# Constant and bias rows from GpSimd's queue, the lists of VectorE and GpSimd behind the T step in another order, and the gates of the T step one slot later

## The chip, the core and the metric

The kernel runs on one core of a Trainium2 chip. The core has TensorE (PE in the rows), VectorE (DVE), ScalarE (ACT), GpSimd (POOL) and SyncE (SP), which here only issues transfers. Each engine works through its own list in order, and they wait for one another through semaphores. The metric is device time in microseconds (us), the median of several runs. Lower is better.

## What is computed

The input x is 8 batches of 128 channels by 256 positions. Self-attention with 16 heads of 8 channels runs on each batch, with a mask on the keys; its result goes through a gated feed-forward block whose activations are rounded to 8-bit integers and whose weights are rounded to -1, 0 or 1; the output of that is added to x.

```
Q, K, V = (proj(Wq), proj(Wk), proj(Wv))
att = einsum('bhqd,bhkd->bhqk', Q, K) / sqrt(8) + b
att = softmax(att * mask + (1 - mask) * NEG_INF)
y = einsum('bhqk,bhkd->bhqd', att, V)
...
h = silu(bit_linear(y, w_gate)) * bit_linear(y, w_up)      # I = 1024
h = rms_norm(h, ln_weight)
out = x + bit_linear(h, w_down)
# bit_linear: activations rounded by their row's maximum, weights by their mean
```

## The kernel before

**Attention, steps n = -1 to 8 of 8 slots (k) each.** Query and key are split into three bf16 parts and stacked over 88 of 128 rows, so that one bf16 matmul gives scores of near float32 accuracy. Batch b lives in `q_st[b % 4]` and `k_st[b % 4]`; the parts get there by small transfers ("high" part 0, "low" parts 1 and 2). Besides the parts a stack has constant rows (ones, or zeros where the maxima will stand) and bias rows (the mask). In slot (n, k) TensorE makes the scores of batch n+1 (`scores`), whose maxima VectorE takes with one reduction a slot (line 938), and the transposed scores of batch n (`scores_t`, the T units), whose exponentials ScalarE takes in two instructions a slot (line 578), and the products with the values (`values`, line 1061). GpSimd turns the maxima into negated bf16 rows (`negate_maxes`), TensorE transposes them (line 1072, at k = 2 and k = 6), ScalarE copies them (line 601), and SyncE moves them into the query stack (line 350). `scores_t` at k = 1 and k = 5 waits for that transfer. Between its pieces of attention GpSimd rounds the weights in steps 4 to 6 (`quantize_weights`, lines 481, 485 and 489, two or three instructions at a time).

**The T step, n = 7 and the start of n = 8.** No scores of a next batch are left. In the place of them units of the feed-forward block run: unit u = 2b + f is half f of batch b. `gate(u)` and `up(u)` are two matmuls each (line 1152); ScalarE takes a tanh or silu of the gate (lines 667 and 676); VectorE multiplies (lines 853, 861, 872, giving `hid`). With one pair of banks for units up to 6, `gate(u)` waits until unit u-1 has been taken out of its bank. `slot_number` s is 0 to 11; before, `gate(s/2)` stands at the end of the even slots, `up` at the end of the odd ones.

**Behind the T step.** For each batch VectorE makes `hid` twice, the upper half of `hw = hid * ln` (line 881, GpSimd makes the lower half, line 512), the row maximum of `hw` (`hidden_maximum`, line 887), the steps of rounding (`hidden_steps`, lines 896 to 900) and the residual (line 917). GpSimd makes the root mean square's inverse and a limit from ScalarE's mean (`hidden_rms`, lines 520 and 522) and the rounding (`round_hidden`, line 530). TensorE transposes that (line 1171), ScalarE copies it (line 700), and `down` (line 1191) gives the output. For the last batch of attention, `scale_y(7)` on VectorE (lines 827, 830, 833) and `quantize_y(7)` on ScalarE (line 610) finish its 8-bit input, and `scale_late_tokens` makes the scales of batches 6 and 7.

All lists are written out by hand; the order in the code is the order on the engine. A number in brackets of a name, as in `hidden_steps(1)`, is the batch.

## Time and profile before

| | us |
|---|---|
| median of 3 runs | 168.88 (168.17 to 168.94) |
| the profiled execution, its own time | 168.71 |
| its span | 166.9 |
| mean granted TensorE clock, share of full speed | 0.969 |

The profiled execution lies 0.17 us below the median, and 1.8 us of its time lie outside the span. The stretches are: start and first scores 0 to 26 us, steps of attention of about 11.6 us each up to 109 us, the T step to about 130 us, the feed-forward block of the remaining batches to the end.

### The profile page before, as it was taken

To read this page: it belongs to the slowest core of one execution; us is meant where nothing else is said; L and a number is where in the kernel's file an instruction comes from. 1 tells how busy PE (TensorE), PEld (TensorE's weight loads), DVE (VectorE), ACT (ScalarE), POOL (GpSimd) and SP (SyncE) were. 2 spreads that over 40 slices of the span, in tenths; PEclk is the share of its full clock that TensorE was granted. 3 is DMA by queue.
4 is the path that set the end of the run, shared out by engine and by line. 5 is a ranking of instruction groups with operands and counts; after the bars stand their busy time and mean duration, and the time that the engine had idled before them with its cause. 6 is when DMAs were issued, how large, how long until landed. Compare 5 with 4: busy or idle time off the path is not lost.

```text
span 166.9 us, 4106 instructions
## 1 busy us (share of the span) xinstructions
PE 147.3 (88%) x1395; PEld 68.8 (41%) x1402; DVE 137.3 (82%) x199; ACT 125.3 (75%) x255; POOL 98.7 (59%) x181
## 2 busy tenths in 40 slices
PE   6969996998999999999999999988789757999883
PEld 3645553433333433433443333323123323766772
DVE  6789997497999989789898998953679666999972
ACT  3041468599899899889889888878699937598970
POOL 5889618508608618508889869523052559779930
PEclk9999999699999999999999999999999995699999
DMA  3984996636246236623322000000000000010112
GB/s 117 299 180 122 266 246 200 161 77 199 57 109 189 45 80 197 182 71 100 76 72 70 0 3 7 5 4 5 0 0 4 0 2 0 0 35 31 33 63 94
DMA packets 20124, 14.19 MB, mean 85 GB/s; under 512 B 2160, under 2 KB 19080, under 8 KB 20104
## 3 DMA queue, kind: packets, MB, share of 16 engines
q1 hardware_dynamic: 17480, 11.76, 25.2%
q10 hardware_dynamic: 2624, 2.17, 4.9%
q8 instruction: 11, 0.18, 0.5%
q14 instruction: 9, 0.07, 0.2%
HBM read 6.17 MB, written 1.07 MB: 43 GB/s over the span
## 4 chain that ended last, share of the span: by engine, by line
PE 61%; ACT 13%; issue 7%; DVE 7%; POOL 5%; ACTq 2%; DMA 2%; DVEq 0%; POOLq 0%
PE y_ps L1061 14%; PE s_ps L1022 13%; ACT probs L578 8%; PE t_ps L1041 6%; PE s_ps L1152 5%; PE t_ps L1171 4%; PE t_ps L998 3%; PE t_ps L1082 3%; PE y_ps L1102 2%; POOL h_m L530 2%; ACTq L286 2%; PE y_ps L1191 2%; PE t_ps L1007 2%; DMA q_st<-nm_rows 2%; PE t_ps L1191 2%
## 5 line engine op out<-in xcount | busy, mean ns | idle before, releaser
L938 DVE TENSOR_REDUCE maxes<-s_ps 128x4 f32<-128x1024 f32 x64 | 75.8, 1217 | 7.8 <-PE s_ps L1022 7.6
L578 ACT ACTIVATE probs<-t_ps 128x512 f32<-128x512 f32 x118 | 65.9, 591 | 10.0 <-PE t_ps L1041 7.8
L1041 PE MATMUL t_ps<-q_st,k_st 64*128 64x256 bf16 x236 | 43.0, 276 | 4.6 <-ACT probs L578 1.9
L1022 PE MATMUL s_ps<-k_st,q_st 64*128 64x256 bf16 x256 | 45.3, 276 | 0.1
L1061 PE MATMUL y_ps<-probs,v_pad 128*18 128x256 f32 x512 | 39.1, 388 | 0.2 <-ACT probs L578 0.2
L1022 PEld LDWEIGHTS s_ps<-k_st,q_st 64*128 64x128 bf16 x256 | 15.9, 94 | 29.0 <-issue 14.7
L1152 PE MATMUL s_ps<-w_q,ffn_x 128*128 128x512 bf16 x59 | 17.5, 396 | 7.3 <-DVE hid L872 4.4
L445 POOL TENSOR_SCALAR nm_parts<-maxes 128x16 bf16<-128x16 f32 x16 | 3.3, 209 | 29.7 <-DVE maxes L938 24.0
L1041 PEld LDWEIGHTS t_ps<-q_st,k_st 64*128 64x128 bf16 x236 | 14.0, 94 | 9.5 <-ACT probs L578 4.3
L512 POOL TENSOR_TENSOR hw<-hid,ln_bc 128x512 f32<-128x512 f32 x8 | 10.2, 1272 | 12.3 <-DVE hid L861 10.4
L1061 PEld LDWEIGHTS y_ps<-probs,v_pad 128*18 128x18 f32 x512 | 9.6, 96 | 13.9 <-issue 11.7
L530 POOL TENSOR_SCALAR h_m<-hw,h_qs 128x1024 f32<-128x1024 f32 x7 | 9.2, 1310 | 5.0 <-DVE h_qs L899 5.0
L1152 PEld LDWEIGHTS s_ps<-w_q,ffn_x 128*128 128x128 bf16 x64 | 4.9, 99 | 16.7 <-issue 12.4
L1171 PE MATMUL t_ps<-ident_f,h_m 128*128 128x128 f32 x64 | 10.4, 294 | 1.3 <-ACT h_T L700 0.5
L700 ACT ACTIVATE h_T<-t_ps 128x512 bf16<-128x512 f32 x16 | 9.1, 596 | 3.2 <-PE t_ps L1171 3.1
L683 ACT ACTIVATE hid_sq<-hid 128x1024 f32<-128x1024 f32 x8 | 8.5, 1056 | 3.8 <-DVE hid L872 3.8
L586 ACT ACTIVATE qk_f<-t_ps 128x512 f32<-128x512 f32 x7 | 4.2, 597 | 9.1 <-PE t_ps L998 5.3
L887 DVE TENSOR_REDUCE h_amax<-hw 128x1 f32<-128x1024 f32 x8 | 9.7, 1208 | 1.4 <-POOL hw L512 1.3
L1171 PEld LDWEIGHTS t_ps<-ident_f,h_m 128*128 128x128 f32 x64 | 8.0, 151 | 4.0 <-issue 2.1
L472 POOL TENSOR_TENSOR parts<-qk_r,parts 128x512 bf16<-128x512 f32 x7 | 8.1, 1160 | 0.6
L468 POOL TENSOR_TENSOR qk_r<-qk_f,parts 128x512 f32<-128x512 f32 x7 | 8.1, 1157 | 0.6
L872 DVE TENSOR_TENSOR hid<-silu_g,s_ps 128x512 f32<-128x512 f32 x12 | 8.1, 678 | 0.2 <-ACT silu_g L676 0.2
(114 smaller groups left out, 242.7 us busy)
## 6 DMA issues: line engine op xcount, KB each, us to landing
q_st<-parts SPq DMA_DIRECT2D x48, 64.0 KB
k_st<-parts SPq DMA_DIRECT2D x33, 64.0 KB
w_f<-in_wgT ACTq DMA_DIRECT2D x2, 512.0 KB, 5.4
w_f<-in_wuT SPq DMA_DIRECT2D x2, 512.0 KB, 4.1
w_f<-in_wdT SPq DMA_DIRECT2D x2, 512.0 KB, 4.3
out<-o_sb SPq DMA_DIRECT2D x8, 128.0 KB, 1.7
k_st<-parts ACTq DMA_DIRECT2D x15, 64.0 KB
x_sb<-in_x SPq DMA_DIRECT2D x2, 256.0 KB, 3.7
```

Of the source, the lines that this page charges most:

```text
L512: pool.tensor_tensor(hw[:, b % 3, 0:512], hid[:, b % 2, 0, :], ln_bc[:, 0:512], ALU.mult)\
L530: pool.tensor_scalar(h_m[:, b % 3, :], hw[:, b % 3, :], h_qs[:, b:b + 1], MAGIC, ALU.mult, ALU.add)\
L578: act.activation(probs[:, t % NP_RING].rearrange("p e t -> p (e t)"), src, ACT.Exp, scale=SCALE)\
L683: act.activation(hid_sq[:, :], hid[:, b % 2].rearrange("p f n -> p (f n)"), ACT.Square, accum_out=h_ssq[:, b:b + 1]).then_inc(sq_done, 1)
L700: act.activation(h_T[:, b % 2, 4 * f:4 * f + 4].rearrange("p a t -> p (a t)"), t_bank(f), ACT.Copy, bias=-MAGIC).then_inc(hT_copied, 1)
L887: dve.tensor_reduce(h_amax[:, b:b + 1], hw[:, b % 3, :], AX.X, ALU.max, apply_absolute_value=True)\
L938: dve.tensor_reduce(dst[:, :, s, :], s_ps[:, c % 2], AX.X, ALU.max).then_inc(s_maxed, 1)
L1022: mm = pe.matmul(s_ps[:, c % 2, i, e, :], q_st[b % RING][rows, hp, qt * P:qt * P + P], k_st[b % RING][rows, hp, :], start=True, stop=True)
L1041: mm = pe.matmul(t_bank(bank["t", t])[:, e * T:e * T + T], k_st[b % RING][rows, hp, kt * P:kt * P + P], q_st[b % RING][rows, hp, :], start ...
L1061: last = pe.matmul(y_ps[32 * j:32 * j + HEAD_COLS, tau * T:tau * T + T], v_pad[:, b, kt, a, (DH + 1) * s:(DH + 1) * s + HEAD_COLS], probs[ ...
L1152: last = pe.matmul(s_ps[:, slot(u), m].rearrange("p a t -> p (a t)"), ffn_x[:, a, b, :], w_q[:, m, a * I + 512 * f:a * I + 512 * f + 512], ...
L1171: last = pe.transpose(t_bank(f)[:, c * P:c * P + P], h_m[:, b % 3, 512 * f + c * P:512 * f + c * P + P], ident_f[:, :])
```

## The change

- SyncE gives up the constant and the bias rows of batches 3 to 7. GpSimd issues them, two transfers a batch, at the end of steps 0 to 4, behind `negate_maxes(n + 1, 0)` (in step 4 ahead of two instructions of rounding weights). They count on semaphores of their own. Rows of batch 2 stay on SyncE, both ahead of the high part.
- `load_high` takes over the waits that a stack is free or cleared.
- The gates of units 1 to 5 move from the end of slot 2u to slot 2u+1, behind its T units and transposes and ahead of its products with the values.
- VectorE: `hidden_steps(1)` ahead of `hidden_maximum(2)`; `scale_y(7)` behind the second half of batch 3; `scale_late_tokens` comes from GpSimd to VectorE right behind it, with five instructions for six.
- ScalarE: `quantize_y(7)` behind the silus of batch 4.

```diff
-LOADS = 2 * len(SPLITS) + 2
+LOADS = 2 * len(SPLITS)
...
         def load_high(queue, b, side):
+            if b >= RING:
+                queue.wait_ge(unit_ready, unit["t", 16 * (b - RING + 1) - 1] + 1)
+            elif b:
+                queue.wait_ge(q_zeroed, b + 1)
+                queue.wait_ge(k_zeroed, b + 1)
             queue.wait_ge(hi_ready, b + 1)
...
+            def load_constant_rows(b):
+                if b < RING:
...
+                    pool.dma_start(q_st[b % RING][BIAS_ROWS], ones6[:, :, :].to_broadcast([6, NHP, T]))\
+                        .then_inc(later_rows_in[b % RING], 16)
+                else:
+                    pool.wait_ge(unit_ready, unit["t", 16 * (b - RING + 1) - 1] + 1)
+                    pool.dma_start(q_st[b % RING][MAX_ROWS], zeros6[:, :, :].to_broadcast([6, NHP, T]))\
+                        .then_inc(later_rows_in[b % RING], 16)
+                pool.wait_ge(bias_stored, 16)
+                pool.dma_start(k_st[b % RING][BIAS_ROWS],
...
                 if has(n + 1):
                     negate_maxes(n + 1, 0)
+                if n >= 0 and has(n + 3):
+                    load_constant_rows(n + 3)
                 for step in weight_steps.get(n, ((), ()))[1]:
                     quantize_weights(step)
...
                         if u == 5:
                             weight_high_half(2)
+                            hidden_steps(1)
...
             hidden_maximum(AHEAD - 1)
-            scale_y(B - 1)
-            hidden_steps(AHEAD - 2)
             for b in range(AHEAD, B):
                 gate_times_up(2 * b)
                 hidden_steps(b - 1)
                 gate_times_up(2 * b + 1)
                 weight_high_half(b)
+                if b == AHEAD:
+                    scale_y(B - 1)
+                    scale_late_tokens()
...
+                    s = slot_number(n, k)
+                    if s > 1 and s % 2:
+                        gate(s // 2)
                     if not has(n + 1):
                         due_values(n, k)
...
-                    s = slot_number(n, k)
-                    if s >= 0 and s % 2 == 0:
-                        gate(s // 2)
+                    if s == 0:
+                        gate(0)
                     if s >= 0 and s % 2:
                         up(s // 2)
```

GpSimd's list at the end of step 4 and the start of step 5 was, with `nm_parts` and `nm_t` the instructions of `negate_maxes` and `w_f`, `w_q` those of rounding weights:

```order
L453 TENSOR_SCALAR nm_parts<-nm_t 128x4x4 [waits nm_step]
L481 TENSOR_SCALAR w_f<-w_f,w_inv 128x2048 [waits abs_done,wscale_step]
L485 TENSOR_SCALAR w_f<-w_f 128x2048 [waits w_rounded]
L445 TENSOR_SCALAR nm_parts<-maxes 128x4x4 [waits unit_ready,s_maxed]
L447 TENSOR_TENSOR nm_t<-maxes,nm_parts 128x16 [waits nm_step]
```

and is now:

```order
L446 TENSOR_SCALAR nm_parts<-nm_t 128x4x4 [waits nm_step]
L494 DMA q_st<-zeros 6x8x256 [waits unit_ready]
L497 DMA k_st<-bias_scr 6x8x256 [waits bias_stored]
L474 TENSOR_SCALAR w_f<-w_f,w_inv 128x2048 [waits abs_done,wscale_step]
L478 TENSOR_SCALAR w_f<-w_f 128x2048 [waits w_rounded]
L438 TENSOR_SCALAR nm_parts<-maxes 128x4x4 [waits unit_ready,s_maxed]
L440 TENSOR_TENSOR nm_t<-maxes,nm_parts 128x16 [waits nm_step]
```

Two transfers now stand ahead of the weights and of the next `negate_maxes`.

VectorE's list behind the T step was, from the upper half of `hw` of batch 2 on:

```order
L881 TENSOR_TENSOR hw<-hid,ln_bc 128x512 [waits hid_done]
L887 TENSOR_REDUCE h_amax<-hw 128x1 [waits high_product,low_product]
L827 TENSOR_REDUCE y_amax<-t_ps 128x1 [waits unit_ready]
L830 TENSOR_SCALAR y_step<-y_amax 128x1 [waits yq_scale]
L833 RECIPROCAL y_qs<-y_step 128x1 [waits yq_scale]
L896 TENSOR_SCALAR h_step<-h_amax,h_lim 128x1 [waits amax_done,hs_pool]
L899 RECIPROCAL h_qs<-h_step 128x1 [waits step_done]
```

and is now, from the same place on and then from `hw` of batch 3 on:

```order
L887 TENSOR_TENSOR hw<-hid,ln_bc 128x512 [waits hid_done]
L902 TENSOR_SCALAR h_step<-h_amax,h_lim 128x1 [waits amax_done,hs_pool]
L905 RECIPROCAL h_qs<-h_step 128x1 [waits step_done]
L906 TENSOR_SCALAR h_os<-h_step,h_rs,u_down 128x1
L893 TENSOR_REDUCE h_amax<-hw 128x1 [waits high_product,low_product]
L878 TENSOR_TENSOR hid<-silu_g,s_ps 128x512 [waits low_product,sq_done,up_ready,silu_done]
```

```order
L887 TENSOR_TENSOR hw<-hid,ln_bc 128x512 [waits hm_done,hid_done]
L820 TENSOR_REDUCE y_amax<-t_ps 128x1 [waits unit_ready]
L823 TENSOR_SCALAR y_step<-y_amax 128x1 [waits yq_scale]
L826 RECIPROCAL y_qs<-y_step 128x1 [waits yq_scale]
L847 TENSOR_SCALAR u_scale<-y_step,w_mean 128x2 [waits yq_scale]
L848 TENSOR_SCALAR u_eps<-y_qs,w_inv 128x2
L850 TENSOR_SCALAR g_scale<-y_step,w_mean 128x2
L852 SCALAR_TENSOR_TENSOR u_sq<-u_scale 128x2 [waits late_scales]
L854 TENSOR_SCALAR u_down<-u_scale,w_mean 128x2
L893 TENSOR_REDUCE h_amax<-hw 128x1 [waits high_product,low_product]
```

The three instructions of `hidden_steps(1)` went ahead of a maximum, and eight small ones now stand between `hw` and the maximum of batch 3.

TensorE's list in slots 4 and 5 of the T step was, with `q_st,k_st` the T units and `w_q,ffn_x` the gate and the up of unit 2:

```order
L1061 MATMUL y_ps<-probs,v_pad 18x256 x3
L1152 MATMUL s_ps<-w_q,ffn_x 128x512 [waits gated,unit_free2]
L1152 MATMUL s_ps<-w_q,ffn_x 128x512
L1041 MATMUL s_ps<-q_st,k_st 128x256 [waits unit_free4,nm_in1]
L1041 MATMUL t_ps<-q_st,k_st 128x256 [waits unit_free0]
L1041 MATMUL s_ps<-q_st,k_st 128x256
L1041 MATMUL t_ps<-q_st,k_st 128x256
L1096 MATMUL t_ps<-ident_f,y_m 128x128 [waits unit_free0,unit_free2]
L1096 MATMUL t_ps<-ident_f,y_m 128x128
```

and is now:

```order
L1073 MATMUL y_ps<-probs,v_pad 18x256 x3
L1053 MATMUL s_ps<-q_st,k_st 128x256 [waits unit_free4,nm_in1]
L1053 MATMUL t_ps<-q_st,k_st 128x256 [waits unit_free0]
L1053 MATMUL s_ps<-q_st,k_st 128x256
L1053 MATMUL t_ps<-q_st,k_st 128x256
L1108 MATMUL t_ps<-ident_f,y_m 128x128 [waits unit_free0,unit_free2]
L1108 MATMUL t_ps<-ident_f,y_m 128x128
L1164 MATMUL s_ps<-w_q,ffn_x 128x512 [waits gated,unit_free2]
L1164 MATMUL s_ps<-w_q,ffn_x 128x512
```

The gate went behind four T matmuls and two transposes.

## Rows read from the trace of the kernel before

**Rows 1.** The page: TensorE's granted clock in 40 slices, tenths of full speed.
```profile
PEclk9999999699999999999999999999999995699999
```

**Rows 2.** Stretches: length, busy PE, PEld, DVE, ACT, POOL, clock, DMA share, GB/s.
```profile
90.90:102.50 11.60, 11.28 (x143) 4.45 (x142) 10.86 (x14) 10.24 (x22) 9.66 (x15) 1.00 0.02 4
```
```profile
130.00:140.00 10.00, 5.94 (x30) 2.94 (x30) 6.83 (x17) 6.04 (x13) 6.34 (x13) 0.89 0.00 1
```

**Rows 3.** Timeline, start: start, length, engine, line, what, [idle before <- releaser].
```profile
23.00 0.36 ACT L601 ACTIVATE nm_rows<-t_ps 24x256 bf16<-24x256 bf16 x1
...
23.39 0.75 SPq L350 DMA_DIRECT2D q_st<-nm_rows  x1
...
26.28 0.28 PE L1041 MATMUL t_ps<-q_st,k_st 64*128 64x256 bf16 x1 [1.26 <-DMA q_st<-nm_rows]
```

**Rows 4.** Transfers by line: ns of issue (smallest/median/largest), first and last start, us.
```profile
L331 SPq DMA_DIRECT2D q_st<-ones x4: 777/790/941, 3.2 to 21.7; - x4
```
```profile
L350 SPq DMA_DIRECT2D q_st<-nm_rows x16: 714/764/791, 23.4 to 115.3; - x16
```

**Rows 5.** Timeline, GpSimd at the end of a step, and around step 5.
```profile
49.88 0.20 POOL L445 TENSOR_SCALAR nm_parts<-maxes 128x16 bf16<-128x16 f32 x1 [4.80 <-DVE maxes L938]
```
```profile
84.50 1.89 POOL L485 TENSOR_SCALAR w_f<-w_f 128x2048 f32<-128x2048 f32 x1
...
86.59 0.21 POOL L445 TENSOR_SCALAR nm_parts<-maxes 128x16 bf16<-128x16 f32 x1 [0.21 <-DVE maxes L938]
...
87.79 0.20 POOL L453 TENSOR_SCALAR nm_parts<-nm_t 128x16 bf16<-128x16 f32 x1
...
88.33 0.28 PE L1072 MATMUL t_ps<-ident_b,nm_parts 128*24 128x128 bf16 x2
...
88.97 2.36 DVE L938 TENSOR_REDUCE maxes<-s_ps 128x4 f32<-128x1024 f32 x2 [0.18 <-PE s_ps L1022]
```

**Rows 6.** Timeline, the T step.
```profile
118.58 0.38 PE L1152 MATMUL s_ps<-w_q,ffn_x 128*128 128x512 bf16 x1 [1.25 <-DVE silu_g L853]
...
119.31 0.60 ACT L578 ACTIVATE probs<-s_ps 128x512 f32<-128x512 f32 x1 [1.57 <-PE t_ps L1041]
...
130.72 0.36 DVE L815 RECIPROCAL y_rec<-t_ps 128x32 f32<-128x32 f32 x1 [1.14 <-PE t_ps L1082]
```

**Rows 7.** Timeline, VectorE and GpSimd behind the T step.
```profile
132.96 1.22 DVE L887 TENSOR_REDUCE h_amax<-hw 128x1 f32<-128x1024 f32 x1
...
134.10 0.41 DVE L827 TENSOR_REDUCE y_amax<-t_ps 128x1 f32<-128x256 f32 x1
...
134.82 0.21 DVE L896 TENSOR_SCALAR h_step<-h_amax,h_lim 128x1 f32<-128x1 f32 x1
...
135.32 1.12 POOL L530 TENSOR_SCALAR h_m<-hw,h_qs 128x1024 f32<-128x1024 f32 x1 [2.25 <-DVE h_qs L899]
...
137.44 0.21 DVE L896 TENSOR_SCALAR h_step<-h_amax,h_lim 128x1 f32<-128x1 f32 x1 [1.45 <-POOL h_lim L522]
...
137.95 0.68 DVE L872 TENSOR_TENSOR hid<-silu_g,s_ps 128x512 f32<-128x512 f32 x1
...
138.66 0.69 DVE L881 TENSOR_TENSOR hw<-hid,ln_bc 128x512 f32<-128x512 f32 x1
...
139.36 1.26 POOL L512 TENSOR_TENSOR hw<-hid,ln_bc 128x512 f32<-128x512 f32 x1
...
140.65 1.22 DVE L887 TENSOR_REDUCE h_amax<-hw 128x1 f32<-128x1024 f32 x1 [1.31 <-POOL hw L512]
```

**Rows 8.** Timeline, five small VectorE instructions: the first and the fifth.
```profile
109.53 0.22 DVE L838 TENSOR_SCALAR g_scale<-y_step,w_mean 128x6 f32<-128x6 f32 x1
...
110.20 0.22 DVE L845 TENSOR_SCALAR u_down<-u_scale,w_mean 128x6 f32<-128x6 f32 x1
```

**Rows 9.** Timeline, the next batches behind the T step.
```profile
143.93 1.61 DVE L881 TENSOR_TENSOR hw<-hid,ln_bc 128x512 f32<-128x512 f32 x1
...
145.86 1.20 DVE L887 TENSOR_REDUCE h_amax<-hw 128x1 f32<-128x1024 f32 x1
```

82 lines of the change are left out of this document (37 added, 45 removed).

## The prediction

> **What bounds the kernel now.** I read the stretches first. In a steady step of 11.60 us VectorE is busy for 10.86 us [rows 2], more than ScalarE and GpSimd; TensorE's 11.28 us are pipelined matmuls with modelled ends and say less. The reader is to see there that VectorE's maxima set the pace of a step, and that an edit which doesn't reach VectorE (or TensorE just ahead of it) is worth nothing in this stage. Behind the T step the picture is another: from 130 to 140 us nobody is busy for more than 6.83 of 10 us [rows 2], so engines wait for each other in a circle. Then the timelines of the three places that the change touches: the first maxima's transfer [rows 3], GpSimd at the ends of steps [rows 5], and the lists of VectorE and GpSimd behind the T step [rows 7]. Last the clock: TensorE is at its upper level (2.4 GHz) but for one slice near 30 us and two from 138 to 146 us [rows 1], where the mean share is 0.6, 0.5 and 0.6.
>
> **SyncE gives up transfers: 0 to -0.5 us, I take -0.1.** On SyncE an issue of the ones costs 0.79 us by the median [rows 4], and I price the bias rows alike, 1.58 us a pair. In the steady steps no row of the views shows TensorE waiting for the stack for longer than its usual gap, and VectorE sets the pace, so these 1.6 us a step are bought from an engine that nobody waits for. At the start the transfer of the first maxima is on the path: TensorE waits 1.26 us for it until 26.28 us. But SyncE issues it at 23.39 us, right behind ScalarE's copy (23.00 + 0.36 = 23.36 us) [rows 3], so the issue can't be earlier. What can change is the landing, 26.28 - 23.39 = 2.89 us with issue, since one transfer fewer is in flight ahead of it. Above I know nothing that makes it longer; below I allow 0.5 us of the 1.26 us. The waits that `load_high` takes over are for events that the rows transfers waited for before.
>
> **GpSimd issues two transfers a batch: +1.5 us, in step 4 alone.** No row of the trace has a transfer issued by GpSimd. The nearest row is the same transfer on SyncE: 1.58 us the pair by the median, and 2 x 0.94 = 1.88 us by the slowest issue of ones [rows 4]. I call the pair D. At the ends of steps 0 to 3 GpSimd then stands idle for `negate_maxes`, 4.80 us in the row [rows 5], which hides any D up to that. In step 4 it has two weight instructions behind the pair. They end at 84.50 + 1.89 = 86.39 us, and GpSimd had only 0.21 us of idle time ahead of the next `negate_maxes`, which ends at 87.79 + 0.20 = 87.99 us; TensorE transposes its result at 88.33 us, in order, ahead of the second half of the scores of that slot; VectorE waits 0.18 us for these and goes on at 88.97 us [rows 5]. So the cover is 0.21 us and at most 0.34 us of handing over, of which I count 0.14 us: a delay of D - 0.35 us goes through TensorE to VectorE, and VectorE, which sets the pace, doesn't get it back. With D = 1.88 us that is 1.53 us. I take the slowest row, since a pair on an engine that issues nothing else is rather like the first than like the median. The bounds: D as low as nothing, if the issue doesn't hold up GpSimd's arithmetic, gives 0; D = 2.9 us gives 2.55 us. That upper end is GpSimd's slowness against VectorE for the same multiplication (1.26 against 0.69 us [rows 7], 1.83 times), put on 1.58 us. Behind it GpSimd is late by D and TensorE by D - 0.35 us, so at the next `negate_maxes` the two stand 0.35 us nearer than before, and no second stall of size comes.
>
> The Trainium skill, page "DMA: Bandwidth & Descriptors", section "Latency and other measured facts", gives about 1 us until the first byte of a transfer from GpSimd, because its cores make the descriptors in software, against about 0.6 us on the other queues. No row here shows it; by that figure D would be an estimated 2.0 us and the delay 1.65 us, and the sum below would end 0.1 us higher. The same page ("Issuing engines are not separate DMA queues") says that issuing from more engines saves only the time of issue, which speaks against this part of the change.
>
> **Gates of the T step a slot later: -0.4 us.** Before, TensorE stands at gate(2) until 118.58 us because VectorE has not taken unit 1 (1.25 us idle); the T units queued behind it keep ScalarE waiting 1.57 us until 119.31 us [rows 6]. Now these T units go first. They wait for the last maxima's transfer, issued at 115.3 us [rows 4]; with the 2.89 us of [rows 3] it lands at about 118.2 us, so ScalarE starts the exponentials near 118.6 us, 0.7 us earlier. Against this each gate is behind four T matmuls, and TensorE's list gets full: gate, products, up and the next T units follow without a gap from about 122.7 us. I walked the list on and kept 0.25 us at the last exponentials and 0.4 us at VectorE's `y_rec`, which stood at 130.72 us after 1.14 us idle [rows 6]. Bounds: -0.8 us (all of the early start kept, and a little more for the transpose of batch 6 that no longer stands behind a gate) and +0.9 us (a gate late by the T units in each of the last units).
>
> **VectorE's and GpSimd's lists: -2.2 us.** The circle before: the maximum of batch 2 (from 132.96 us), `scale_y` (134.10 us), `hidden_steps(1)` (134.82 us), GpSimd's rounding (135.32 us, after 2.25 us idle), its root and limit, `hidden_steps(2)` (137.44 us, after 1.45 us idle), `hid` of unit 7 (137.95 us), its `hw` (138.66 us). Meanwhile GpSimd does the late scales and only then, at 139.36 us, the lower `hw` of batch 3, for which VectorE's next maximum waits 1.31 us until 140.65 us [rows 7].
> - `hidden_steps(1)` goes past a maximum and `scale_y`: 134.82 - 132.96 = 1.86 us earlier, plus the 0.4 us of the T step, so it starts near 132.6 us.
> - The circle behind it keeps its length (137.95 - 134.82 = 3.13 us to `hid` of unit 7), since GpSimd was waiting for exactly this: unit 7 at about 135.7 us, its `hw` done at 135.7 + 0.68 + 0.7 = 137.1 us.
> - `scale_y` (134.82 - 134.10 = 0.72 us) and the late scales stand there now. Five like instructions took 110.20 + 0.22 - 109.53 = 0.89 us [rows 8]. The maximum of batch 3 starts at 137.1 + 0.72 + 0.89 = 138.7 us. GpSimd's lower `hw` can start at about 135.2 us without the late scales ahead of it and is done by then; the wait of 1.31 us is gone. Gain at this point 140.65 - 138.7 = 1.95 us, 0.4 us of it the T step's.
> - From this maximum to the next the kernel took 145.86 - 140.65 = 5.21 us [rows 9, 7], of which 1.61 us are a `hw` that takes 0.69 us where GpSimd's rounding doesn't run beside it [rows 9, 7]. GpSimd's rounding of batch 3 now starts earlier against it, and ScalarE and TensorE are ahead by the same shift. I count 0.65 us of the 0.92 us, since two engines that alternate will still meet somewhere. Behind it the batches repeat, and the gain is carried to the end.
>
> That is 1.55 + 0.65 = 2.2 us beside the 0.4 us. Bounds: 1.2 us (nothing of the last point, 0.35 us lost to a collision) to 2.6 us.
>
> **The sum** against the profiled execution's own 168.71 us: -0.1 + 1.53 - 0.4 - 2.2 = -1.2 us, 167.5 us. The median of before lies 0.17 us above that execution, which is less than the error of any term, and I leave the number as it is.
>
> **The rivals.**
> - GpSimd's arithmetic is not held up by the pair, or so little that 0.35 us cover it. For it: nothing in the trace shows the contrary. Against it: transfers hold up SyncE for 0.71 us and more each [rows 4]. It gives 168.71 - 2.7 = 166.0 us.
> - Slower: the pair is dear. If D is 3.5 us or more, TensorE stands still for over 3 us in step 5, and its clock falls behind that. Such a thing is seen at the start: a wait of 1.26 us until 26.28 us [rows 3] is followed by the slice at 0.6 [rows 1]. Price: 3.2 us, plus 1 us for a slice at the lower level, less 2.7 us: 170.2 us. It decides from D = 4.1 us, or 3.1 us with the fall of the clock (168.71 - 2.7 + D - 0.35 past 169.7 us, less that 1 us); from there the kernel is slower by over 0.5%.
> - The tail gives most back. TensorE stays at the lower level from 138 to 146 us as before [rows 1], and VectorE's upper `hw` of batch 3 now meets GpSimd's rounding of batch 2, as that of batch 4 did at 143.93 us for 1.61 us instead of 0.69 us [rows 9, 7]. Then 0.9 us and 0.9 us of the 2.6 us are lost: 167.5 + 1.8 = 169.3 us, or 168.4 us with one of the two.
> - The T step gets longer: the later gates cost 0.9 us instead of giving 0.4 us, 168.8 us.
>
> The Trainium skill, page "SBUF — State Buffer", section "Who interferes with whom", has VectorE instructions with two inputs in SBUF and GpSimd's reads lock each other out for a whole instruction; by that rule the second of two that meet waits, whichever it is, which the 1.61 us agree with, and the collision is a matter of where the two lists stand.
>
> **How the numbers follow.** A measurement of this kernel can tell about 0.5%, 0.84 us, from no change; so faster is below 168.0 us and slower above 169.7 us. Forecast 0.41 (166.8 to 168.2 us; 0.34 of it faster, 0.07 same). Pair hidden 0.20 (165.4 to 166.6 us, 0.19 faster). Pair dear 0.16 (169.4 to 172 us, 0.15 slower). Tail gives back 0.15 (168.4 to 169.3 us, 0.02 beyond on the slow side). T step longer 0.08 (same). Faster 0.34 + 0.19 = 0.53, slower 0.15 + 0.02 = 0.17, the rest 0.30. The range leaves out the lowest 0.05 of the second case and nearly all of the third: 165.6 to 169.5 us.
>
> **What would show it.** The pair: GpSimd's row of `negate_maxes` in step 5 later than its maxima, a wait of TensorE's transpose (line 1072 before) for it of about 1.5 us, and a step longer by that. The gates: exponentials of pair 60 waiting under 1 us and `y_rec` nearer to the last step of attention than the 21.2 us from 109.53 to 130.72 us. The lists: GpSimd's first rounding behind the T step about 2.3 us earlier against `y_rec`, no wait of the maximum of batch 3 for GpSimd, and 13 us instead of 15.1 us from `y_rec` to the maximum of batch 4. What would make it wrong: an issue on GpSimd of under 0.3 us or over 1.5 us, a fall of the clock in a place where none was, or a wait of ScalarE's silu of batch 4 that moves into the place of the one removed.

## The result and the profile after

The changed kernel took 163.74 us (median of 4 executions, 162.91 to 165.66), beside 168.52 us for the kernel before (median of 4, 167.66 to 168.94). The ratio is 0.971, 95% interval 0.962 to 0.979. Here and below all executions count in the medians and ranges, while those over 1.5% above the fastest of the same kernel are left out of the ratios. The forecast was 167.5 us, in a range from 165.6 to 169.5 us: the sign was right, the size was not, and the time lies below the range. The profiled execution took 163.05 us, 5.66 us less than that of before, and its span is 161.2 us instead of 166.9.

The page of the changed kernel: granted clock, and the DMA queue that is new (packets, MB, share of 16 engines).

```profile
PEclk9999999999999999999999999999999999999999
...
q0 software_dynamic: 320, 0.25, 1.0%
```

Two things are seen. GpSimd's transfers are there (q0, 320 packets). And TensorE's clock, which before fell in a slice near 30 us and in two from 138 us on [rows 1], doesn't fall at all in this execution. Whether the change did that is half of the story below.

The same stretches as in [rows 2], of the changed kernel: length, busy PE, PEld, DVE, ACT, POOL, clock, DMA share, GB/s.

```profile
90.00:101.60 11.60, 11.28 (x142) 4.45 (x142) 11.09 (x14) 10.24 (x22) 10.15 (x15) 1.00 0.01 3
128.00:138.00 10.00, 6.75 (x42) 3.87 (x41) 8.94 (x24) 7.29 (x16) 7.16 (x10) 1.00 0.00 1
```

The steady step is what it was. In the ten microseconds behind the T step VectorE is now busy for 8.94 us instead of 6.83: the circle of waits is partly undone.

The timeline of the changed kernel around step 5, GpSimd and VectorE (against [rows 5]): start, length, engine, line, what, [idle before <- releaser].

```profile
80.78 0.62 POOL L494 DMA_DIRECT2D q_st<-zeros  x1
81.41 0.56 POOL L497 DMA_DIRECT2D k_st<-bias_scr  x1
...
86.04 0.21 POOL L438 TENSOR_SCALAR nm_parts<-maxes 128x16 bf16<-128x16 f32 x1
...
87.59 0.27 PE L1084 MATMUL t_ps<-ident_b,nm_parts 128*24 128x128 bf16 x2 [0.86 <-POOL nm_parts L446]
...
88.22 2.35 DVE L944 TENSOR_REDUCE maxes<-s_ps 128x4 f32<-128x1024 f32 x2 [1.10 <-PE s_ps L1034]
```

The pair is 0.62 + 0.56 us of GpSimd's time. GpSimd has no idle left ahead of the maxima of step 5, TensorE waits 0.86 us for its result, and VectorE 1.10 us instead of 0.18 us for TensorE. The chain is the one that was forecast, the price is not.

The T step of the changed kernel (against [rows 6]):

```profile
114.24 0.72 SPq L350 DMA_DIRECT2D q_st<-nm_rows  x1
...
116.12 1.21 ACT L570 ACTIVATE probs<-s_ps 128x512 f32<-128x512 f32 x2
...
116.30 0.28 PE L1053 MATMUL s_ps<-q_st,k_st 64*128 64x256 bf16 x1
...
117.22 0.59 ACT L570 ACTIVATE probs<-t_ps 128x512 f32<-128x512 f32 x1
...
128.21 0.36 DVE L808 RECIPROCAL y_rec<-t_ps 128x32 f32<-128x32 f32 x1 [1.14 <-PE t_ps L1094]
```

The first T unit that needs the last maxima starts 2.06 us after their transfer was issued, without a wait. Its exponential is the second of ScalarE's two from 116.12 us on, and ScalarE has lost its 1.57 us of idle time.

Behind the T step, changed kernel (against [rows 7]):

```profile
130.60 0.21 DVE L902 TENSOR_SCALAR h_step<-h_amax,h_lim 128x1 f32<-128x1 f32 x1 [0.25 <-POOL h_lim L533]
...
133.22 0.21 DVE L902 TENSOR_SCALAR h_step<-h_amax,h_lim 128x1 f32<-128x1 f32 x1 [0.32 <-POOL h_lim L533]
...
133.72 0.68 DVE L878 TENSOR_TENSOR hid<-silu_g,s_ps 128x512 f32<-128x512 f32 x1
134.43 0.69 DVE L887 TENSOR_TENSOR hw<-hid,ln_bc 128x512 f32<-128x512 f32 x1
...
136.34 0.22 DVE L854 TENSOR_SCALAR u_down<-u_scale,w_mean 128x2 f32<-128x2 f32 x1
136.47 1.21 DVE L893 TENSOR_REDUCE h_amax<-hw 128x1 f32<-128x1024 f32 x1
```

VectorE's wait of 1.45 us is down to 0.32 us and that of 1.31 us is gone, the late scales stand on VectorE, and the maximum of batch 3 starts at 136.47 us instead of 140.65.

I cut each trace at seven points of VectorE's list: the first `y_rec` (batch 0), `y_rec` of batches 3 and 4, `g_scale` (end of attention), the last `y_rec`, the maximum of batch 3, and the last residual. The stretches between these points that the table leaves out moved by no more than 0.1 us in this pair.

| stretch, us | before | after | difference |
|---|---|---|---|
| start to first `y_rec` | 43.64 | 41.97 | -1.67 |
| `y_rec` of batch 3 to batch 4 (step 5) | 11.55 | 12.18 | +0.63 |
| `g_scale` to last `y_rec` (T step) | 21.19 | 19.73 | -1.46 |
| last `y_rec` to maximum of batch 3 | 9.93 | 8.26 | -1.67 |
| maximum of batch 3 to last residual | 23.58 | 22.07 | -1.51 |

### The profile page after: what moved, and what is told of

Same layout as the page of the kernel before. It is cut to its first block, busy times and chain, and to the rows that moved or that the text cites. A ratio compares the mean times of both kernels' runs of the same rounds, so it can differ in the third digit from the quotient of the medians.

```text
span 161.2 us, 4126 instructions
## 1 busy us (share of the span) xinstructions
PE 143.8 (89%) x1402; PEld 66.7 (41%) x1402; DVE 136.7 (85%) x204; ACT 125.4 (78%) x255; POOL 104.0 (65%) x185
## 4 chain that ended last, share of the span: by engine, by line
PE 55%; DVE 12%; ACT 11%; POOL 8%; issue 7%; DMA 4%; SPq 1%; ACTq 0%; DVEq 0%; POOLq 0%
PE y_ps L1073 14%; PE s_ps L1034 13%; ACT probs L570 5%; PE t_ps L1053 5%; DVE maxes L944 4%; PE s_ps L1164 4%; PE t_ps L1006 3%; DMA bias_scr<-bias_parts 2%; PE t_ps L1094 2%; ACT hid_sq L675 2%; PE y_ps L1114 2%; PE t_ps L1183 2%; PE t_ps L1015 2%; DVE hid L878 2%; PE t_ps L1203 2%
## 5 line engine op out<-in xcount | busy, mean ns | idle before, releaser
L1034 PE MATMUL s_ps<-k_st,q_st 64*128 64x256 bf16 x256 | 44.7, 274 | 1.0 <-DMA k_st<-bias_scr 0.5
L1053 PE MATMUL t_ps<-q_st,k_st 64*128 64x256 bf16 x236 | 42.5, 274 | 3.3 <-ACT probs L570 1.6
L1073 PE MATMUL y_ps<-probs,v_pad 128*18 128x256 f32 x512 | 38.6, 384 | 0.2 <-ACT probs L570 0.2
L541 POOL TENSOR_SCALAR h_m<-hw,h_qs 128x1024 f32<-128x1024 f32 x7 | 10.1, 1447 | 3.2 <-DVE h_qs L905 3.2
L1183 PE MATMUL t_ps<-ident_f,h_m 128*128 128x128 f32 x64 | 9.5, 276 | 2.0 <-ACT h_T L692 1.3
L1183 PEld LDWEIGHTS t_ps<-ident_f,h_m 128*128 128x128 f32 x64 | 7.3, 141 | 4.2 <-POOL h_m L541 2.3
L1114 PE MATMUL y_ps<-idle_rows 128*128 128x512 bf16 x24 | 7.5, 435 | 1.3 <-POOL idle_rows L400 1.3
```

The source lines that it names most:

```text
L541: pool.tensor_scalar(h_m[:, b % 3, :], hw[:, b % 3, :], h_qs[:, b:b + 1], MAGIC, ALU.mult, ALU.add)\
L1034: mm = pe.matmul(s_ps[:, c % 2, i, e, :], q_st[b % RING][rows, hp, qt * P:qt * P + P], k_st[b % RING][rows, hp, :], start=True, stop=True)
L1053: mm = pe.matmul(t_bank(bank["t", t])[:, e * T:e * T + T], k_st[b % RING][rows, hp, kt * P:kt * P + P], q_st[b % RING][rows, hp, :], start ...
L1073: last = pe.matmul(y_ps[32 * j:32 * j + HEAD_COLS, tau * T:tau * T + T], v_pad[:, b, kt, a, (DH + 1) * s:(DH + 1) * s + HEAD_COLS], probs[ ...
L1114: pe.matmul(y_ps[:, :], idle_rows[:, 0:P], idle_rows[:, :], start=True, stop=True)
L1183: last = pe.transpose(t_bank(f)[:, c * P:c * P + P], h_m[:, b % 3, 512 * f + c * P:512 * f + c * P + P], ident_f[:, :])
```

## The experiments

Two theories. **A**: the parts add up: transfers +0.63 us in step 5, gates -1.46, lists -1.67, and the rest of the difference, in the start and behind the maximum of batch 3, is TensorE's clock. **B**: the gains come from another part than I think, or by chance from one execution to the next. The last five columns are the stretches of the table above, from one profiled execution of each kernel.

| kernel | median us (n), lowest | ratio to before, 95% | start | step 5 | T step | to max. 3 | to the end |
|---|---|---|---|---|---|---|---|
| transfers only | 167.84 (10), 165.92 | 0.996 [0.990, 1.001] | 43.27 | 12.20 | 21.19 | 9.93 | 23.13 |
| gates only | 165.95 (10), 164.80 | 0.991 [0.987, 0.995] | 41.89 | 11.55 | 19.73 | 9.93 | 23.58 |
| lists only | 165.11 (4), 163.69 | 0.984 [0.977, 0.992] | 43.17 | 11.55 | 21.19 | 8.27 | 22.25 |
| last rows on SyncE | 162.57 (4), 162.00 | 0.974 [0.966, 0.982] | 43.93 | 11.55 | 19.73 | 8.27 | 22.08 |
| tail filler | 167.19 (12), 165.70 | 0.999 [0.995, 1.003] | 41.60 | 11.56 | 21.19 | 9.92 | 22.59 |
| start filler | 166.75 (12), 165.66 | 0.998 [0.994, 1.002] | 41.72 | 11.55 | 21.19 | 9.92 | 22.60 |
| without transfers part | 163.96 (6), 163.39 | 0.982 [0.977, 0.988] | 42.06 | 11.55 | 19.72 | 8.25 | 22.23 |
| changed, again | 162.58 (6), 162.32 | 0.974 [0.969, 0.979] | 41.39 | 12.18 | 19.73 | 8.27 | 22.06 |
| both fillers | 167.28 (12), 165.68 | 0.999 [0.994, 1.003] | 41.67 | 11.55 | 21.18 | 9.92 | 22.57 |
| last rows on SyncE, again | 162.45 (6), 161.71 | 0.968 [0.962, 0.974] | 41.97 | 11.55 | 19.73 | 8.26 | 22.07 |
| last rows later | 162.29 (6), 162.10 | 0.969 [0.963, 0.976] | 41.36 | 11.55 | 19.73 | 8.26 | 22.06 |
| changed, third | 162.66 (6), 162.32 | 0.971 [0.965, 0.977] | 41.43 | 12.16 | 19.73 | 8.26 | 22.07 |

The kernel before ran beside the first four with a median of 167.46 us (19 executions, lowest 166.24), beside the next four with 167.35 (23, lowest 165.46), beside the last four with 168.24 (17, lowest 165.85).

### Each part alone

Transfers only:

```
             for n in range(FIRST, LAST + 1):
...
                 if has(n + 1):
                     negate_maxes(n + 1, 0)
+                if n >= 0 and has(n + 3):
+                    load_constant_rows(n + 3)
```

with SyncE's list as in the diff of the change.

> The kernel before with the transfers part of the change alone (constant and bias rows of batches 3 to 7 from GpSimd's queue, SyncE's list rearranged); the order of the gates and of the late lists is that of before. Theory A (the start gained because SyncE's list lets TensorE run without the dip of its clock near 30 us, and GpSimd's pair costs only some 0.6 us of step 5): y_rec of the first quantized batch near 42.0 us instead of 43.6, the end of attention 1.0 us earlier, 167.5 us against 168.5. Rival B (the gain of the start is chance or comes from the other parts; the pair costs 0.6 to 1.5 us): the start stays at 43.6 and the time is 169.0 to 170.0 us.

Measured: 12.20 us in step 5, so +0.65 us there, and everything behind it as before. The start was 43.27 us with the clock at half near 30 us. Theory A's 42.0 us did not come in this execution: this part doesn't keep the clock up there.

Gates only:

```
+                    s = slot_number(n, k)
+                    if s > 1 and s % 2:
+                        gate(s // 2)
...
-                    s = slot_number(n, k)
-                    if s >= 0 and s % 2 == 0:
-                        gate(s // 2)
+                    if s == 0:
+                        gate(0)
```

> The kernel before with the gates of the T-step units a slot later and nothing else. Theory A (the T step gained 1.46 us because the last batch's exponentials no longer find TensorE late): the distance from g_scale to y_rec of the last batch falls from 21.19 to about 19.8 us, and the time to 167.1 us; the start and the tail as in the kernel before. Rival B (the T step's gain comes from work that the lists moved out of it): the distance stays near 21 us and the time at 168.5 us.

Measured: the T step falls to 19.73 us, the whole 1.46 us. The start was 41.89 us, although its code is that of before: a start of 42 us doesn't need the transfers part.

Lists only (`scale_late_tokens` from GpSimd to VectorE, `hidden_steps(1)` ahead of the maximum, `scale_y` and `quantize_y` of the last batch behind unit 7):

```
                         if u == 5:
                             weight_high_half(2)
+                            hidden_steps(1)
...
             hidden_maximum(AHEAD - 1)
-            scale_y(B - 1)
-            hidden_steps(AHEAD - 2)
...
                 weight_high_half(b)
+                if b == AHEAD:
+                    scale_y(B - 1)
+                    scale_late_tokens()
```

> The kernel before with the reordered lists of VectorE, GpSimd and ScalarE behind the T step and nothing else. Theory A (the lists earn 1.67 us up to the maximum of batch 3, and what follows gains up to 1.2 us as the collision at the next hidden product is gone): 165.7 us. Rival B (the second 1.2 us is owed to TensorE's clock not falling near 140 us, which this part alone does not bring): 166.9 us, with a low granted clock in that stretch.

Measured: 8.27 us to the maximum of batch 3, the whole 1.66 us, and 22.25 us from there on, 1.33 us less than in the first trace of before. Theory A holds for both; B expected a low clock there and there was none.

The three ratios come to -0.4, -0.9 and -1.6%, together -2.9%, which is what the whole change does (0.971). By the stretches the parts add up, and none of them hides another. By the ratios that is shown only as far as their intervals reach, which are 0.4 to 0.8 points to either side; the interval of the transfers part takes in no change at all.

### The pair of transfers in step 5

```
+                if n == 4:
+                    sp.wait_ge(unit_ready, unit["t", 16 * (n + 3 - RING + 1) - 1] + 1)
+                    sp.dma_start(q_st[3][MAX_ROWS], zeros6[:, :, :].to_broadcast([6, NHP, T]))\
+                      .then_inc(rows7_in, 16)
...
-                if n >= 0 and has(n + 3):
+                if n >= 0 and has(n + 3) and n < 4:
                     load_constant_rows(n + 3)
```

> The changed kernel, but the two transfers of the last batch's constant and bias rows issued from SyncE's queue behind the hand-over of the maxima in step 4, as the kernel before had them, with a semaphore of their own; batches 3 to 6 stay on GpSimd. Theory A (the 1.10 us for which VectorE waits in step 5 are the two issues of 0.62 and 0.57 us on GpSimd): no such wait, and 0.6 to 0.9 us less than the changed kernel. Rival B (the wait is that of GpSimd's other work, or SyncE's issue delays the maxima as much): the same time as the changed kernel within 0.3 us.

The timeline of this kernel, GpSimd and VectorE in step 5:

```profile
84.79 1.89 POOL L486 TENSOR_SCALAR w_f<-w_f 128x2048 f32<-128x2048 f32 x1
86.89 0.21 POOL L446 TENSOR_SCALAR nm_parts<-maxes 128x16 bf16<-128x16 f32 x1 [0.21 <-DVE maxes L952]
...
89.27 2.36 DVE L952 TENSOR_REDUCE maxes<-s_ps 128x4 f32<-128x1024 f32 x2 [0.18 <-PE s_ps L1044]
```

GpSimd's 0.21 us and VectorE's 0.18 us of idle time are those of [rows 5] again, and step 5 takes 11.55 us. So the wait of 1.10 us is the pair and nothing else. A shorter edit does nearly the same: the pair stays on GpSimd and goes behind the maxima of step 5.

```
                 if has(n):
                     negate_maxes(n, 1)
+                if n == 5:
+                    load_constant_rows(7)
...
-                if n >= 0 and has(n + 3):
+                if n >= 0 and n < 4:
                     load_constant_rows(n + 3)
```

> The changed kernel, but the last batch's two row transfers stay on GpSimd and are issued behind the maxima of step 5, so ahead of no maxima that VectorE's buffers wait for. Theory A (their 1.19 us cost only because they stand ahead of the weights' two long operations and the maxima of step 5): 11.55 us in step 5, 0.6 us less than the changed kernel. Rival B (the weights' operations take the same time from the maxima of step 6 instead): a wait of VectorE in a later step, and no gain.

> The changed kernel with the last batch's two row transfers back in SyncE's queue, again, beside the changed kernel: 11.55 us instead of 12.18 in step 5, all else the same; 0.6 us faster in the median if the start and the clock fall alike in both.

> The changed kernel itself, the scale for the two kernels above: 12.18 us in step 5, 19.73 in the T step, 8.26 to the maximum of batch 3, 22.07 from there to the end; only the start differs from one execution to another (41.4 to 43.9 us).

Measured side by side: medians of 162.29 us (later), 162.45 (SyncE) and 162.66 (the changed kernel), so 0.4 and 0.2 us where 0.6 was expected. In the traces step 5 takes 11.55 us in both, instead of 12.16; with the later pair the next step takes 11.89 instead of 11.56 us, so 0.3 of the 0.6 us come back as rival B had it, since the weights' operations end later:

```profile
86.33 0.57 POOL L497 DMA_DIRECT2D k_st<-bias_scr  x1
...
88.82 1.97 POOL L474 TENSOR_SCALAR w_f<-w_f,w_inv 128x2048 f32<-128x2048 f32 x1
90.75 0.20 POOL L438 TENSOR_SCALAR nm_parts<-maxes 128x16 bf16<-128x16 f32 x1
...
92.92 1.23 DVE L946 TENSOR_REDUCE maxes<-s_ps 128x4 f32<-128x1024 f32 x1 [0.53 <-PE s_ps L1036]
```

Both are ahead of the changed kernel by their traces; their timed intervals overlap with its own, so 0.2 to 0.6 us is as much as can be said, and that they are faster at all is not shown by the times.

### What the transfers part is worth elsewhere

> The changed kernel without its transfers part: gates a slot later and the reordered lists, all constant and bias rows from SyncE's queue as before. Theory A (the transfers part gives the start nothing and costs 0.63 us in step 5): no wait of VectorE in step 5 (18 ns idle groups aside), 91.56 - 80.01 = 11.55 us from y_rec of batch 3 to that of batch 4, time 0.5 to 0.7 us below the changed kernel. Rival B (the transfers part gives the start up to 1.7 us): 1 us above the changed kernel.

Measured: no wait in step 5, as theory A had it, and yet 1.4 us more than the changed kernel in the median (163.96 against 162.58 us), which is rival B's time. One cause is in the trace, in a step that I had not thought of: from `y_rec` of batch 2 to that of batch 3 it took 13.27 us instead of 12.56, since TensorE waited 0.77 us for a transfer of maxima at 67.74 us. The gates-only kernel had the same there (13.09 us). I took it for a matter of an early start that meets a full SyncE queue, and profiled that kernel once more:

> The kernel before with the gates alone a slot later, a second look. Theory A (with all rows on SyncE its queue runs without a gap from 56 to 66 us and hands the maxima of batch 3 over too late when the start was fast): with the first y_rec near 42 us again about 0.5 us more than 12.56 us in step 3 and a wait of TensorE for that transfer; with a first y_rec after 43 us none. Rival B (it was chance): 12.56 us even after a fast start. The tail: 23.6 us if the fall of the clock there is usual with the lists of before, 22.6 if not.

Measured: 12.56 us after a start of 42.72 us, which decides nothing. But one of three further profiled executions of the kernel before (the second, below) had it with a late start, 43.23 us. Its timeline, SyncE's queue and TensorE:

```profile
57.46 3.18 SPq L286 DMA_DIRECT2D k_st<-parts  x3
60.68 0.77 SPq L350 DMA_DIRECT2D q_st<-nm_rows  x1
...
61.98 0.75 SPq L342 DMA_DIRECT2D k_st<-bias_scr  x1
...
64.04 1.23 SPq L286 DMA_DIRECT2D k_st<-parts  x2
65.32 0.60 SPq L286 DMA_DIRECT2D q_st<-parts  x1
65.96 0.61 SPq L286 DMA_DIRECT2D k_st<-parts  x1
66.61 0.78 SPq L350 DMA_DIRECT2D q_st<-nm_rows  x1
...
68.92 0.28 PE L1041 MATMUL t_ps<-q_st,k_st 64*128 64x256 bf16 x1 [0.59 <-DMA q_st<-nm_rows]
```

With the two rows left out here, eight rows of issues follow each other with hardly a gap, and the maxima stand behind them: ScalarE's copy ended at 65.32 us, and the issue comes 1.29 us later. In the changed kernel, without the bias and constant rows, SyncE is done with the same transfers earlier and waits for the maxima (its groups end at 61.83 us, ScalarE's copy ends at 63.23 us, and the transfer is issued at 63.26 us):

```profile
61.23 0.60 SPq L288 DMA_DIRECT2D k_st<-parts  x1
63.26 0.78 SPq L350 DMA_DIRECT2D q_st<-nm_rows  x1
```

Those are of its second profiled execution. Of 11 traces with these rows on SyncE 3 have the late maxima (0.53 to 0.71 us each), of 7 with the rows on GpSimd none. That it happens after an early start only is refuted. A group of issues that takes long adds to it, as the 3.18 us for three of the `k_st` parts above, where three usually take 1.8 to 1.9 us; what makes an issue take long is open.

The same thing happens earlier, at the third transfer of maxima, near 38 us. The lists-only kernel, with its rows on SyncE:

```profile
33.09 3.44 SPq L286 DMA_DIRECT2D k_st<-parts  x3
...
33.85 0.36 ACT L582 ACTIVATE nm_rows<-t_ps 24x256 bf16<-24x256 bf16 x1
...
36.57 0.78 SPq L350 DMA_DIRECT2D q_st<-nm_rows  x1
...
38.50 0.28 PE L1038 MATMUL t_ps<-q_st,k_st 64*128 64x256 bf16 x1 [0.84 <-DMA q_st<-nm_rows]
```

The maxima were issued 2.36 us behind ScalarE's copy, and TensorE waited 0.84 us for them. The changed kernel, second profiled execution:

```profile
31.95 1.81 SPq L288 DMA_DIRECT2D k_st<-parts  x3
...
33.19 0.36 ACT L593 ACTIVATE nm_rows<-t_ps 24x256 bf16<-24x256 bf16 x1
...
33.81 0.78 SPq L350 DMA_DIRECT2D q_st<-nm_rows  x1
```

Here it is 0.26 us, and no wait. Of the 11 traces with the rows on SyncE 4 have such a wait, of 0.28 to 0.84 us; their maxima were issued 0.80 to 2.36 us behind the copy. Their first `y_rec` comes 16.4 to 17.1 us after the first T unit, where it is 15.7 to 16.0 us in the traces with neither this wait nor a low clock nor the start filler below. In the 7 traces with the rows on GpSimd the issue comes 0.02 to 0.35 us behind the copy, and none has the wait. Taken together, 6 of 11 traces have late maxima in one place or the other, against none of 7, which would come out in about 1 case of 40 if the rows made no difference. So SyncE does stand on the path now and then, and the transfers part most likely buys that off. With the clock up throughout, the first `y_rec` comes at 42.2 us on average with the rows on SyncE (10 traces) and at 41.6 us without (5), so this is worth about 0.6 us in the start and 0.2 us in step 3. The times say more: at a mean granted clock of 1.0 the kernel without the transfers part takes 163.9 us and the changed one 162.7 us (means of 5 executions each), where the shares from the traces, less the 0.6 us of step 5, would make about 0.2 us. The other 1 us is open.

### TensorE's clock: the start and the tail

Tail filler and start filler, on the kernel before:

```
                     transpose_hidden(0, 1)
+                    pe.wait_ge(y_raw_ready, B)
+                    keep_array_busy(5)
...
                     gate_and_up(2 * b + 2)
+                    if b == AHEAD:
+                        keep_array_busy(6)
```

> The kernel before, plus eleven matmuls on idle rows (results unused) in the two stretches at 134.8 to 136.1 and 137.2 to 138.8 us in which TensorE waited for VectorE behind the T step: five and then six, about 0.22 us each at full clock. All lists as before. Theory A (what the lists earned behind the maximum of batch 3, 1.3 us, is TensorE's clock, which was granted at half from 138 to 144 us after this idle time): the granted clock stays at 1.0 there, and the distance from the maximum of batch 3 to the last residual falls from 23.58 to about 22.3 us; the time 1.0 to 1.3 us below the kernel before. Rival B (it is the end of the collision of VectorE and GpSimd at the hidden product of batch 4, or the order of the lists): the clock is up or not, the distance stays at 23.3 to 23.6 us.

```
+                if pair == 0 and i == 1 and e == 0:
+                    keep_array_busy(4)
                 if w % 4 == 0 and i == 1 and e == 0:
```

> The kernel before, plus four matmuls on idle rows (results unused) ahead of the transposed scores of pair 0, near 25.2 us, where TensorE waits 0.3 to 1.7 us for the first transfer of maxima. Theory A (the start is 1.5 us longer where TensorE's clock falls to half from 28 to 32 us, and it falls for the idle time of that wait): the clock stays at 1.0 there, y_rec of batch 0 near 42.0 us, time 0.5 to 1.5 us below the kernel before as a median, and less spread. Rival B (the fall comes by chance, whatever TensorE did before): a low clock at 28 to 32 us again, or times spread and centred as those of the kernel before.

> The kernel before, plus both sets of matmuls on idle rows (four ahead of the transposed scores of pair 0, five and six behind the T step; results unused). Theory A (TensorE's clock falls for the idle time in these places): full clock in both, y_rec of batch 0 near 41.7 us, 22.6 us from the maximum of batch 3 to the last residual, and a median of its times near the lowest times of the kernel before, 166.0 us, instead of 167.4. Rival B (fillers of this size don't decide it; the falls come by chance, or for other gaps): times spread and centred as those of the kernel before.

Measured: all three traces have the full clock everywhere, a start of 41.6 to 41.7 us and 22.6 us behind the maximum of batch 3. But the start filler's trace has the full clock in the tail as well, where it adds nothing, and the times of all three are spread like those of the kernel before, from 165.7 to 170 or 171 us, with ratios of 0.998 to 0.999.

The mean granted clock, which is on record for every timed execution, tells more than the three traces. It was 1.0 in 25 of the 36 executions with fillers (7, 8 and 10 of 12), and in 12 of the 59 of the kernel before that ran beside all the experiments. So the fillers did make the falls rarer, and the idle time that they fill has a part in them. What they did not do is shorten the kernel: at a clock of 1.0 the 25 take 165.7 to 169.0 us, mean 166.9, and the 12 take 165.5 to 167.4 us, mean 166.6. The clock is one reason for the spread of the times and not the only one, and as a cure for the time the fillers failed.

> The kernel before itself, one more profiled execution. Theory A (its TensorE clock falls to half behind the T step in most executions, as in the first trace, and the reordered lists end that): 23.1 to 23.6 us from the maximum of batch 3 to the last residual, a granted clock of 0.5 in that stretch. Rival B (the falls come alike in both kernels): 22.6 us and full clock in most looks.

> As the look before it: of three, theory A expects two or three with the fall behind the T step, rival B none or one (none of eight traces with the reordered lists has it).

> As the two looks before it. For the start both theories expect two levels of the first y_rec, 41.4 to 42.1 and 43.2 to 43.9 us, the later ones with a granted clock near 0.5 between 28 and 32 us.

Measured, start and tail: 41.93 and 23.25 us, 43.23 and 22.58, 42.32 and 22.56. One tail of three, not the two or three that theory A expected. The stretches of the first trace of before and then of the first of these three, one and the same kernel:

```profile
28.00:32.00 4.00, 4.00 (x26) 1.90 (x24) 2.50 (x3) 2.55 (x6) 3.49 (x8) 0.57 0.44 108
```

```profile
28.00:32.00 4.00, 4.00 (x45) 1.87 (x44) 3.24 (x4) 3.54 (x8) 3.49 (x8) 1.00 0.39 113
138.00:142.00 4.00, 3.03 (x16) 2.47 (x15) 2.75 (x6) 3.01 (x8) 3.89 (x5) 0.57 0.00 0
```

TensorE had waited 1.26 us for the first maxima in the one [rows 3] and 1.25 us in the other. Behind the first wait the clock is at its lower level (1.2 GHz) for most of four microseconds (26 matmuls are in the row instead of 45), behind the second it stays at the upper one (2.4 GHz). So the clock near 30 us is drawn anew in each execution, for both kernels: it fell in 1 of 11 traces with the rows on SyncE and in 2 of 7 with the rows on GpSimd, and these three have the first `y_rec` at 43.3 to 43.9 us. The expectation that every late start has a low clock was wrong: 43.17 us (lists only) and 43.23 us (the second of the three) came with the clock at 1.00 there, and both have the late third maxima of the section above. In all, the start takes 41.6 to 43.6 us in the 11 traces (mean 42.4) and 41.4 to 43.9 us in the 7 (mean 42.2).

In the tail the draw is not the same. TensorE's two waits there, in the first trace of before and then in the third of the changed kernel:

```profile
136.14 1.02 PE L1152 MATMUL s_ps<-w_q,ffn_x 128*128 128x512 bf16 x3 [1.39 <-DVE hid L872]
138.77 1.86 PE L1152 MATMUL s_ps<-w_q,ffn_x 128*128 128x512 bf16 x4 [1.61 <-DVE hid L872]
```

```profile
132.47 1.02 PE L1164 MATMUL s_ps<-w_q,ffn_x 128*128 128x512 bf16 x3 [0.81 <-DVE hid L878]
133.96 1.02 PE L1164 MATMUL s_ps<-w_q,ffn_x 128*128 128x512 bf16 x4 [0.47 <-DVE hid L878]
```

The first two are 1.39 or 1.40 us and 1.59 to 1.61 us in all 8 traces with the lists of before and no filler there, with a fall behind them or without. With these lists and no filler behind the T step 5 of 8 traces have the fall (23.13 to 23.58 us to the end, mean 23.37) and 3 don't (22.56 to 22.60). With the new lists none of 8 has it (22.06 to 22.25). If the lists made no difference, five of the eight with the old ones and none of the others would come out in about 1 case of 80. The timed executions agree: the mean granted clock was 1.0 in 14 of 79 with the lists of before and no filler, and in 36 of 42 with the new ones. So the new lists keep TensorE at its upper level there, most likely because the two waits are shorter, and that is worth about 5/8 x 0.8 = 0.5 us on average.

The Trainium skill, page "TensorE: Matmul & The Clock Gate", section "Part 1: The HAM clock gate", says that the chip watches TensorE's activity in a window that runs free of the program, so that one kernel can come out differently from run to run. The two rows of 28 to 32 us above agree with it: the same wait, once with a fall behind it and once without.

### The collision that cost nothing

> The changed kernel itself, beside the others, to set the scale. If the start of 41.97 us in its profiled execution was the lucky one of two levels that both kernels have, another execution may have 43.3 to 43.9 us there; all later stretches as before: 12.18 us in step 5, 19.73 us in the T step, 8.26 us to the maximum of batch 3, 22.07 us from there to the last residual.

That second execution of the changed kernel gives the same stretches within 0.02 us, and a start of 41.39 us: the 41.97 was not its best.

The fifth term of the forecast rested on a collision: 1.61 us for VectorE's `hw` of batch 4 [rows 9]. The kernel before, behind it:

```profile
143.93 1.61 DVE L881 TENSOR_TENSOR hw<-hid,ln_bc 128x512 f32<-128x512 f32 x1
...
147.28 0.69 DVE L872 TENSOR_TENSOR hid<-silu_g,s_ps 128x512 f32<-128x512 f32 x1 [0.22 <-ACT silu_g L676]
```

The gates-only kernel, with the same lists and a like clock (0.66 over these 6.63 us, where the kernel before had 0.70):

```profile
141.44 0.69 DVE L881 TENSOR_TENSOR hw<-hid,ln_bc 128x512 f32<-128x512 f32 x1
...
144.79 0.69 DVE L872 TENSOR_TENSOR hid<-silu_g,s_ps 128x512 f32<-128x512 f32 x1 [1.14 <-ACT silu_g L676]
```

There the `hw` takes 0.69 us, VectorE is 0.92 us earlier, and waits 0.92 us longer for ScalarE's silu. From the maximum of batch 3 to this `hid` both take 6.63 us (147.28 - 140.65, 144.79 - 138.16), and 23.58 us to the end. With the full clock (start filler) it is 144.37 - 138.73 = 5.64 us. VectorE waited for ScalarE in both, and the length goes with TensorE's clock: of the ten traces with the lists of before (those with fillers too) the five with the fall have 6.30 to 6.63 us here and the five without 5.62 to 5.64 us. The collision only filled a wait. It was also the exception. In all ten GpSimd's rounding starts 0.04 us ahead of this `hw`, and in nine of them, the gates-only kernel's too, it is the rounding that gets longer (1.64 instead of 1.12 us) and the `hw` takes 0.69 us. The forecast had read the one execution in which it was the other way round.

## Why the prediction was wrong

At equal clock the change is worth 3.0 us from the first `y_rec` on. Take the third further execution of the kernel before and the third trace of the changed one, both at the upper level throughout: from the first `y_rec` to the last residual 161.85 - 42.32 = 119.53 us against 157.97 - 41.43 = 116.54 us, which is -2.99 = +0.61 (step 5) -1.46 (T step) -1.66 (to the maximum of batch 3) -0.49 (to the end) +0.01. The lowest times of each, 165.46 and 162.32 us, differ by 3.14 us. The forecast sum was -1.2. Three steps of it failed, and all three made the gain too small: the landing of the last maxima (gates, 1.1 us), the price of the pair on GpSimd (0.9 us), and that nobody waits for SyncE (about 0.7 us). Term by term:

- **SyncE gives up transfers, -0.1 us.** About 0.7 us too small: by the traces it is -0.6 us in the start and -0.2 us in step 3 at equal clock, and by the times perhaps more. The step that failed is the one that said no row shows TensorE waiting for the stack or SyncE in the steady steps, so nobody waits for SyncE. In that trace nobody did; in 6 of 11 TensorE did, at the third maxima or in step 3. And the term looked at the first maxima alone, where SyncE was not late. One trace shows which queue is full, not how near to late it is.
- **GpSimd's pair, +1.53 us.** The mechanism, the place and the cover of 0.35 us were right: the extra wait of VectorE is 1.10 - 0.18 = 0.92 us for D = 1.18 us, and D - 0.35 would be 0.83. The size of D was wrong: I took SyncE's slowest row, 2 x 0.94 us, and GpSimd takes 0.62 + 0.56. That a first pair on an engine is slow holds for that first one alone (below). And VectorE did get some back: 0.92 us of wait became 0.63 us of step, where I had said none. Together 0.9 us too dear.
- **Gates, -0.4 us.** The largest miss, 1.06 us. The step that failed is the landing at 118.2 us, from the 2.89 us of the first maxima's transfer, which runs beside the weight loads (DMA share 0.73 from 26 to 28 us). At 114 us no other transfer is being issued, and it took at most 2.06 us. Then the exponentials of pair 60 don't wait at all (1.57 us gone, not 0.7), and of this 1.46 us arrive at the last `y_rec`, where I had let 0.7 us shrink to 0.4 for a list that gets full. No row stood behind that either.
- **Lists up to the maximum of batch 3, -1.55 us.** Right: -1.66 to -1.67, in the changed kernel and alone. The circle keeps its length: 3.12 us (133.72 - 130.60) where it was 3.13.
- **Lists behind it, -0.65 us.** The number was near (-0.33 alone, -0.49 with the rest, at equal clock), by luck, for the reason was wrong: the collision cost nothing and came in 1 of 10 traces. What brings the 0.33 to 0.49 us I didn't separate. Beside it there is the fall of the clock, 0.8 us where it comes, which the new lists seem to prevent. I had the low clock among the rivals, as something that stays. It is the reason why the term looked like -1.5 us in the first pair of traces.

What is left: 163.74 against 168.52 us is -4.8 us, the two later comparisons gave -4.8 and -5.6 us of median. At equal clock the traces give 3.0 us from the first `y_rec` on, about 0.6 us in the start and 0.2 us for the late maxima of step 3, together 3.8 us. The timed executions with a mean granted clock of 1.0 agree: 12 of the kernel before take 166.6 us on average and 11 of the changed kernel 162.8 us, 3.8 us less. Over all executions of these the means differ by 4.5 us (167.6 us over 59, 163.1 us over 12), so the clock adds about 0.7 us: it was below 1.0 in 47 of the 59 and in 1 of the 12. The traces place 0.5 us of that in the tail. That the medians differ by more than the means, up to 1.1 us, lies within the intervals of the ratios (3.5 to 5.2 us and 3.9 to 5.8 us in the later comparisons), and what the executions of 169 and 170 us look like no trace shows.

Of the rivals, "pair hidden" (166.0) was nearer than the forecast, but not for its reason. "Tail gives back" was the wrong way round: its clock went up. That collision did move, as it says: VectorE's `hw` of batch 3 at 134.43 us meets GpSimd's rounding. But it is GpSimd's instruction that gets longer:

```profile
131.10 1.12 POOL L541 TENSOR_SCALAR h_m<-hw,h_qs 128x1024 f32<-128x1024 f32 x1 [0.54 <-DVE h_qs L905]
...
134.38 1.64 POOL L541 TENSOR_SCALAR h_m<-hw,h_qs 128x1024 f32<-128x1024 f32 x1
```

1.64 instead of 1.12 us, and two small instructions later GpSimd has 1.38 us of idle time. In both kernels the collision lies where somebody waits anyway.

The range was too narrow for a plain reason: its lower end, 165.6, took in one favourable bound at a time. Pair at 0.63, gates at -0.8 and lists at -2.6 together would have been 165.8 us, and gates at what they were 165.2. And all of it was put against one execution (168.71 us) that had the clock down twice, worth 1.0 us in its tail (23.58 against 22.57 us) and had a start 1.2 us over the mean of 42.4.

## What to carry to other kernels

Before a stretch is costed from one trace, look which of its rows stand at a lower clock: a gain or a loss there may be drawn anew in the next execution, and sums should be made between points that lie outside of it. A queue that nobody waited for in one trace can still be near to late: compare the end of what a transfer waits for with its issue, in several executions. A transfer's landing time belongs to the traffic beside it: take it from a row with the same DMA share. An instruction that a collision has stretched costs something only if the next one on its engine doesn't wait; two rows below it settle that.
